# MLP's first weights and input made in the last group of the first attention, and another order of small work in the second attention

## The chip, the cores and the metric

One core of one Trainium2 chip runs the whole program in one launch. The metric is the device time of that launch in microseconds (us). Five engines work side by side and meet at semaphores: TensorE (PE; its weight loads are shown as PEld), VectorE (DVE), ScalarE (ACT), GpSimd (POOL) and SyncE (SP, which here only issues transfers).

## What is computed

Two transformer layers in fp32 on 2 x 1024 tokens of width 256. Each of the four parts has the same frame, x + layernorm(part(layernorm(x))):

```python
x = x + _layernorm(_L0_attn_ref(_layernorm(x), ...))   # 16 heads of 128, weights = codes * scales, full softmax
x = x + _layernorm(_L0_ffn_ref(_layernorm(x), ...))    # silu(x @ gate.T * gs) * (x @ up.T * us) @ down.T * ds, 704 hidden
x = x + _layernorm(_L1_attn_ref(_layernorm(x), ...))   # 16 heads of 16, causal softmax
x = x + _layernorm(_L1_ffn_ref(_layernorm(x), ...))    # 2 shared experts + top 8 of 16 routed ones, 128 hidden each
```

## The kernel before

**Precision.** A fp32 product is made from a high and a low part of each operand, in three matmuls (`three_passes`; `project` does it for both halves of the 256 channels). So each operand is split first: ACT copies it to its high part, then DVE (if the source is in PSUM) or POOL (if in SBUF) subtracts for the low part. `take_hi` and `take_lo` do it for the input of a stage, after `turn` on PE has transposed it.

**Norm.** The 16 tiles of 128 tokens are 4 groups of 4. For one group, a norm after a part is: statistics of the part's result `acc` (DVE, `stats_acc`), scale and offset (POOL, `scale_acc`), `normalise_acc` (ACT), add to x and statistics of x (DVE, `add_up`), `scale_x` (POOL), `normalise_x` (ACT), then `turn`, `take_hi`, `take_lo` into `xT`. norm1 stands between the first attention and the MLP, norm3 between the second attention and the experts.

**First attention** (`attention0_stage`). Two heads a pass, two sequences a pass. In the last one, norm1 of groups 0 and 1 is woven in by `begin_norm`; their x rows are loaded then, and the MLP's first 128 hidden units (`first_part`) with them. After the last tile PE runs `weighted_v` in four parts (o of the last group) with `output` of the group before between them. Then ACT and DVE split o, and `output` of the last group runs in two halves through one PSUM bank, bank 7. DVE does acc statistics of group 2 ahead of reading the first half (lines 960 to 964). The stage ends with a barrier of all engines.

**MLP** (`Mlp0.block`). 24 steps: 6 slices of 128 hidden units (`e`) for each of 4 token groups (`c`). PE runs `gate_up(s+1)` (12 matmuls of 512 columns), then `down(s)` (12 of 256). Ahead of the first, it turns input group 0, and ACT and DVE split it. Slices are split by `split_hi` (ACT) and `split_lo` (POOL), slices 0 and 1 first, slice s+2 in step s. Group 1 is turned in step 1, groups 2 and 3 in steps 6 and 10. Steps 7 and later carry parts of norm2 and the second attention's first projections (`Early`).

**Second attention** (`attention1_stage`). 8 halves (4 heads of one sequence each) of 12 quads; step g of 96 does quad g. In a step PE makes scores of quad g+2 into a ring of 4 PSUM banks, peaks for a later half into 3 other banks, and weighs v; ACT takes exp, DVE the peaks. `small_work` names by quad what else is done: `project`, `stack` (q and k spread to 64 rows; four a chunk of 512 tokens), `shift` (adds the peaks), `sums`, `spread` and `out` (end of a head group's result). Each of them takes one ring bank, in order, so it waits for what used this bank four places earlier. POOL's `make_y` (4 instructions) lies between spread and out.

**Experts** (`Moe`) begin inside the last steps: the router's logits, `sigmoid`, the best 8 (`find_best`, `take_best`), the weights (`weigh_best`, 7 small DVE instructions in a row); step p of the experts is g = TOTAL + p, and there PE runs `gate_up(p+1)` and `down(p)`, and DVE `product(p+1)` and `add_up(p)`, with `hidden_hi` (ACT) and `hidden_lo` (POOL) between.

## Time and profile before

| | |
|---|---|
| median of 3 runs | 2249.73 us (2246.76 to 2250.08) |
| profiled execution, its own time | 2251.21 us |
| its span, first to last instruction | 2249.5 us |
| mean granted TensorE clock | 0.971 |
| first attention, up to its last instruction | 1354.8 us |
| MLP, to the second attention's first matmul | 1355.2 to 1498.9 us |
| second attention, to its last o | up to 1900.3 us |

Of the profile, the page gives shares by engine, the timeline gives instructions of one engine in order of time, and the view of waits gives sums of them. In a timeline a line is: start (us), duration (us), engine, source line, operation, what it writes <- what it reads, sizes, count of merged instructions, and in brackets how long the engine stood idle before it and what ended that.

### The profile page before, as it was taken

To read this page: it belongs to the slowest core of one execution; us is meant where nothing else is said; L and a number is where in the kernel's file an instruction comes from. 1 tells how busy PE (TensorE), PEld (TensorE's weight loads), DVE (VectorE), ACT (ScalarE), POOL (GpSimd) and SP (SyncE) were. 2 spreads that over 40 slices of the span, in tenths; PEclk is the share of its full clock that TensorE was granted. 3 is DMA by queue.
4 is the path that set the end of the run, shared out by engine and by line. 5 is a ranking of instruction groups with operands and counts; after the bars stand their busy time and mean duration, and the time that the engine had idled before them with its cause. 6 is when DMAs were issued, how large, how long until landed. Compare 5 with 4: busy or idle time off the path is not lost. (4 is left out here: it accounts for less than half of the span.)

```text
span 2249.5 us, 35911 instructions
## 1 busy us (share of the span) xinstructions
PE 2122.8 (94%) x12680; PEld 1710.5 (76%) x12680; DVE 1468.5 (65%) x2625; ACT 1186.2 (53%) x2159; POOL 565.8 (25%) x558
## 2 busy tenths in 40 slices
PE   6999999999999999999999998989889898899996
PEld 5888888888888888888888877764455445788885
DVE  6676676676676676676667775446766782655555
ACT  5565465465465465455556555526656764433333
POOL 3021031031031031021021005412333443544443
PEclk9999999999999999999999998988999997999998
DMA  2010010010010010010020002000000010110001
GB/s 81 1 41 2 1 41 2 1 41 2 1 40 2 1 41 2 1 41 2 1 41 29 1 10 73 1 8 4 4 4 6 1 36 15 36 36 22 22 1 38
DMA packets 37687, 41.03 MB, mean 18 GB/s; under 512 B 7936, under 2 KB 33408, under 8 KB 37504
## 3 DMA queue, kind: packets, MB, share of 16 engines
q1 hardware_dynamic: 37504, 38.57, 6.4%
q8 instruction: 118, 1.93, 0.4%
q14 instruction: 65, 0.53, 0.1%
HBM read 36.45 MB, written 2.10 MB: 17 GB/s over the span
## 5 line engine op out<-in xcount | busy, mean ns | idle before, releaser
L816 ACT ACTIVATE attn_probT_hi<-psum 128x512 fp32r<-128x512 f32 x512 | 278.4, 595 | 305.9 <-PE psum L678 305.9
L874 DVE TENSOR_REDUCE attn_neg_max<-psum 128x1 f32<-128x1024 f32 x256 | 313.1, 1223 | 193.0 <-PE psum L81 192.4
L931 DVE TENSOR_TENSOR attn_probT_lo<-psum,attn_probT_hi 128x512 fp32r<-128x512 f32 x512 | 327.2, 680 | 28.0 <-ACT attn_probT_hi L816 27.9
L790 ACT ACTIVATE attn_prob<-psum,attn_neg_max 128x1024 f32<-128x1024 f32 x256 | 286.7, 1120 | 6.5 <-DVE attn_neg_max L874 6.5
L678 PEld LDWEIGHTS psum<-ident_sb,attn_prob 128*128 128x128 f32 x2048 | 237.8, 141 | 61.9 <-DVE attn_probT_lo L931 13.3
L678 PE MATMUL psum<-ident_sb,attn_prob 128*128 128x128 f32 x2048 | 267.4, 274 | 11.2 <-ACT attn_prob L790 11.2
L607 POOL TENSOR_TENSOR attn_v_lo<-x_sb,attn_v_hi 128x512 fp32r<-128x512 f32 x64 | 82.0, 1281 | 762.1 <-ACT attn_v_hi L824 762.1
L81 PE MATMUL psum<-attn_probT_hi,attn_v_hi 128*128 128x512 f32 x512 | 212.3, 415 | 0.6 <-DVE attn_probT_lo L931 0.6
L2216 ACT ACTIVATE attn_probT<-psum 128x512 f32<-128x512 f32 (+3 forms) x384 | 163.9, 495 | 92.2 <-PE psum L2101 89.2
L81 PE MATMUL psum<-attn_key_hi,attn_q_lo 128*128 128x512 f32 x512 | 201.0, 393 | 9.8 <-issue 9.8
L81 PE MATMUL psum<-attn_key_hi,attn_q_hi 128*128 128x512 f32 x512 | 201.4, 393 | 4.9 <-DVE xT_lo L348 4.9
L81 PE MATMUL psum<-attn_probT_lo,attn_v_hi 128*128 128x512 f32 x512 | 201.3, 393 | 0.0
L81 PE MATMUL psum<-attn_key_lo,attn_q_hi 128*128 128x512 f32 x512 | 200.7, 392 | 0.0
L81 PE MATMUL psum<-attn_probT_hi,attn_v_lo 128*128 128x512 f32 x512 | 200.4, 391 | 0.0
L1783 DVE TENSOR_REDUCE attn_peaks<-psum 128x1 f32<-128x512 f32 (+1 forms) x256 | 155.9, 651 | 47.7 <-PE psum L1747 26.0
L891 DVE SCALAR_TENSOR_TENSOR acc_sb<-psum,attn_over_total,acc_sb 128x256 f32<-128x256 f32 x256 | 111.7, 478 | 59.8 <-PE psum L81 54.1
L1422 POOL TENSOR_TENSOR attn_qk_lo<-attn_moe_hidden,attn_qk_hi 128x512 fp32r<-128x512 f32 x72 | 93.3, 1296 | 176.6 <-ACT attn_qk_hi L1386 176.6
L1449 DVE TENSOR_TENSOR attn_moe_hidden<-psum,attn_v 128x512 f32<-128x512 f32 x72 | 49.7, 690 | 134.0 <-ACT attn_v L1380 113.0
L81 PE MATMUL psum<-xT_hi,attn_q 128*128 128x512 f32 x288 | 116.8, 406 | 6.5 <-POOL attn_key L1418 6.5
L81 PE MATMUL psum<-xT_hi,attn_w_hi 128*128 128x512 f32 x288 | 117.3, 407 | 3.2 <-POOL attn_bias_v L560 2.1
L2101 PE MATMUL psum<-attn_q,attn_key 64*128 64x512 f32 (+3 forms) x384 | 106.1, 443 | 11.3 <-DVEq L2287 4.2
L1462 DVE SCALAR_TENSOR_TENSOR acc_sb<-psum,moe_weigh,acc_sb 128x256 f32<-128x256 f32 x272 | 112.9, 477 | 5.3 <-PE psum L81 5.1
(222 smaller groups left out, 4855.0 us busy)
## 6 DMA issues: line engine op xcount, KB each, us to landing
attn_v_all<-in_moe_w SPq DMA_DIRECT2D x23, 384.0 KB, 3.0
acc_sb<-in_x SPq DMA_DIRECT2D x4, 512.0 KB, 6.0
x_sb<-in_wq_codes SPq DMA_DIRECT2D x8, 256.0 KB, 2.5
x_sb<-in_wq_scales SPq DMA_DIRECT2D x32, 64.0 KB, 3.0
x_sb<-in_wk_codes SPq DMA_DIRECT2D x8, 256.0 KB, 3.8
x_sb<-in_wk_scales SPq DMA_DIRECT2D x32, 64.0 KB, 4.5
x_sb<-in_wv_codes SPq DMA_DIRECT2D x8, 256.0 KB, 5.1
x_sb<-in_wv_scales SPq DMA_DIRECT2D x32, 64.0 KB, 5.6
```

The source lines that it names most:

```text
L81: ins = nc.tensor.matmul(out, stationary[s], moving[m], start=start and n == 0, stop=stop and n == len(PASSES) - 1)
L678: mm = nc.tensor.transpose(ring(use)[:, j * P:(j + 1) * P], prob[:, i % 2, kt * P:(kt + 1) * P], k.ident[:])
L790: nc.scalar.activation(prob[:, i % 2, :], scores(i).rearrange("p a b -> p (a b)"), ACT.Exp, bias=neg_max[:, i % 2:i % 2 + 1], accum_out=to ...
L816: nc.scalar.activation(probT[0][:, g % 2, half_tile * GT:(half_tile + 1) * GT, j * P:(j + 1) * P], ring(use).rearrange("p (t n) -> p t n", ...
L874: nc.vector.tensor_reduce(neg_max[:, i % 2:i % 2 + 1], scores(i), AX.XY, ALU.max, negate=True).then_inc(max_ready, 1)
L891: add = nc.vector.scalar_tensor_tensor(out=to, in0=out_bank[:, j * C:(j + 1) * C], scalar=over_total[:, g * GT + t:g * GT + t + 1], in1=to ...
L931: nc.vector.tensor_tensor(to[1], ring(use).rearrange("p (t n) -> p t n", n=P), f32(to[0]), ALU.subtract).then_inc(ring_free, 1)
L1422: self.nc.gpsimd.tensor_tensor(self.hid[1][p % 2], self.hidden[p % 2], f32(self.hid[0][p % 2]), ALU.subtract).then_inc(self.lo_done, 1)
L1462: ins = self.nc.vector.scalar_tensor_tensor(out=acc, in0=self.down_tile(j), scalar=by, in1=acc, op0=ALU.mult, op1=ALU.add)
L1783: nc.vector.tensor_reduce(to[:, h:h + 1], bank[:, 0:width], AX.X, ALU.max, negate=True).then_inc(max_free, 1)
L2101: nc.tensor.matmul(score_bank(n)[:, q0:], key[half % 2][pair][rows(h), kt * P:(kt + 1) * P], q[half % 2][pair][rows(h), c * NB + q0:(c + 1 ...
L2216: nc.scalar.activation(probT[:, slot(g, h), q0:], score_bank(g * HG + h)[:, q0:], ACT.Exp, scale=float(D1) ** -0.5).then_inc(exp_done, 1)
```

## The change

What it does, in four parts.

1. *The last group of the first attention.* PE turns input groups 0 and 1 between the parts of `weighted_v`, into banks 2 to 5. ACT runs a Silu on a 128x1 tile, makes the high part of MLP slice 0 and takes the high parts of both input groups; DVE multiplies the down columns of slices 0 and 1 by their scale and takes the low parts; POOL makes the low part of slice 0. The parts of slice 0 lie in the still free columns of `xT`. Slice 1 is loaded where x of group 2 was. The last `output` uses a second bank, bank 1, for its second half. Norm1's acc statistics, scale and normalise of group 2 leave this stage.
2. *MLP.* PE begins with `gate_up(0)`. Slice 1 is split first, the permanent copy of slice 0 in step 4. Group 2's acc work comes to the beginning; x of groups 2 and 3 is loaded after the splits of slices 1 and 0; its steps move from X_ADD 1, 3 to 3, 7, the turns from 1, 6, 10 to 7, 11. SP issues the second attention's constants behind the load of group 3.
3. *Second attention.* The c = 1 stacks of the next half move from quads 2 and 3 to 0 and 1; the c = 0 projection of the half after it from quad 7 to 3, its weights' split from quad 2 to 1.
4. *Beginning of the experts.* Sigmoid from step 92 to 94, best from 93 to 95, weights from 94 to 97 (experts' step 1), `hidden_hi(0)` from 95 to 96, behind the last copy of o. `make_y` of the last chunk in two parts, two instructions in each of experts' steps 1 and 2.

```diff
@@ attention0_stage
+        out_bank, last_out_bank = k.psum[:, 7, :], k.psum[:, 1, :]
+        last_turn_banks = lambda g: k.psum[:, 2 + g * KC:2 + (g + 1) * KC, :]
...
-            ahead(sp)
+            mlp.load_first(sp)
             sp.wait_ge(v_done, passes * 2 * v_uses + 2)
-            for g in range(after.ahead, after.groups - 1):
-                after.load_x(sp, g)
+            mlp.load_second(sp)
...
-            after.early_gpsimd(pool, after.ahead)
+            mlp.first_lo(pool, first_hi)
...
                 for part in range(GT):
                     weighted_v(half, groups - 1, part)
+                    if beside:
+                        beside(part)
                     if 1 <= part <= 2:
                         output(half, groups - 2, part - 1)
+            def begin_mlp(part):
+                if part < after.ahead:
+                    after.turn(pe, part, last_turn_banks(part)).then_inc(after.turned, 1)
...
+            def begin_mlp():
+                nc.scalar.activation(neg_max[:, 0:1], neg_max[:, 0:1], ACT.Silu)
+                mlp.first_hi(act, first_scaled, first_hi)
+                for g in range(after.ahead):
+                    act.wait_ge(after.turned, g + 1)
+                    after.take_hi(act, g, last_turn_banks(g))
-            after.early_scalar(act, after.ahead)
...
                 for part in range(2):
                     add_up(half, b, groups - 2, part)
+                    if beside:
+                        after.take_lo(dve, part, last_turn_banks(part))
                 o_lo(half, groups - 1)
+                if i == tiles - 1:
+                    mlp.scale_first(dve, first_scaled)
-            after.early_vector(dve, after.ahead)
@@ Mlp0
+    def scale_first(self, dve, done):
+        self.scale_down(self.first_part, self.first_row).then_inc(done, 1)
+        self.scale_down(self.second_part, self.first_row)
+    def first_hi(self, act, scaled, done):
+        act.wait_ge(scaled, 1)
+        self.nc.scalar.activation(self.first_halves[0], self.first_part, ACT.Copy).then_inc(done, 1)
+    def first_lo(self, pool, hi_done):
+        self.nc.gpsimd.tensor_tensor(self.first_halves[1], self.first_part, f32(self.first_halves[0]), ALU.subtract)
...
-        X_ADD, X_STATS, X_ACT, X_TURN = {1: 2, 3: 3}, {2: 2, 5: 3}, {4: 2, 7: 3}, {1: 1, 6: 2, 10: 3}
+        X_ADD, X_STATS, X_ACT, X_TURN = {3: 2, 7: 3}, {4: 2, 8: 3}, {5: 2, 9: 3}, {7: 2, 11: 3}
+        SPLIT = {-1: 1, 0: 2, 1: 3, 2: 4, 3: 5, 4: 0}
...
-                for e in range(1, N):
+                for e in range(2, N):
                     sp.dma_start(staged[:, e - 1, :], self.w_dram[e]).then_inc(self.landed[min(e, 3)], 16)
+                sp.wait_ge(w_ready, 1)
+                before.load_x(sp, before.groups - 2)
                 sp.wait_ge(row_kept, 1)
-                sp.wait_ge(w_ready, 1)
+                sp.wait_ge(w_ready, N)
                 before.load_x(sp, before.groups - 1)
                 early.sync(sp)
...
-                turn(before, "x", 0)
                 gate_up(0)
@@ attention1_stage
-        1: [("shift", 0, 1, 0), ("sums", -1, 1, 0)],
-        2: [("spread", -1, 1, 0), ("stack", 1, 1, 0), ("stack", 1, 1, 1)],
-        3: [("stack", 1, 1, 2), ("stack", 1, 1, 3)],
+        0: [("stack", 1, 1, 0), ("stack", 1, 1, 1)],
+        1: [("shift", 0, 1, 0), ("sums", -1, 1, 0), ("stack", 1, 1, 2), ("stack", 1, 1, 3)],
+        2: [("spread", -1, 1, 0)],
+        3: [("project", 2, 0, 0)],
...
-        7: [("project", 2, 0, 0)],
...
-    LAST_Y, LAST_OUT = 1, 4
+    LAST_Y, LAST_OUT = (TOTAL + 1, TOTAL + 2), 4
-    ROUTER_AT, LOGITS_AT, SIGMOID_AT, BEST_AT, WEIGH_AT = 84, range(TOTAL - 8, TOTAL - 4), TOTAL - 4, TOTAL - 3, TOTAL - 2
+    ROUTER_AT, LOGITS_AT, SIGMOID_AT, BEST_AT, WEIGH_AT = 84, range(TOTAL - 8, TOTAL - 4), TOTAL - 2, TOTAL - 1, TOTAL + 1
...
-                if r == 2 and 0 <= half + 2 < HALVES:
+                if r == 1 and 0 <= half + 2 < HALVES:
                     split_weights(pool, half + 2)
...
-                if g == TOTAL - 1:
+                if g == TOTAL:
                     act.wait_ge(stacked, HALVES * chunks * 2 * pairs)
                     moe.hidden_hi(act, 0)
```

## Rows read from the trace of the kernel before

**Rows 1.** The page's first part: busy time, share of the span, instructions.
```profile
PE 2122.8 (94%) x12680; PEld 1710.5 (76%) x12680; DVE 1468.5 (65%) x2625; ACT 1186.2 (53%) x2159; POOL 565.8 (25%) x558
```

**Rows 2.** PE's timeline around the end of the first attention.
```profile
1349.28 0.38 PE L81 MATMUL psum<-attn_wo_hi,attn_o_hi 128*128 128x256 f32 x1 [1.41 <-DVE attn_o_lo L879]
1352.27 0.58 PE L81 MATMUL psum<-attn_wo_hi,attn_o_hi 128*128 128x256 f32 x1 [2.02 <-DVE acc_sb L891]
1355.16 1.94 PE L334 MATMUL psum<-ident_sb,acc_sb 128*128 128x128 f32 x8 [1.24 <-PEq L422]
1359.70 0.77 PE L81 MATMUL psum<-xT_hi,mlp_w_hi 128*128 128x512 f32 x1 [2.59 <-DVE xT_lo L348]
...
1374.32 1.03 PE L334 MATMUL psum<-ident_sb,acc_sb 128*128 128x128 f32 x8
```

**Rows 3.** Windows: length; busy PE, PEld, DVE, ACT, POOL; PEclk; DMA share; GB/s.
```profile
1347.87:1352.20 4.33, 0.97 (x7) 0.77 (x6) 3.56 (x14) 0.60 (x1) 0.89 (x1) 0.90 0.00 0
...
1359.70:1364.90 5.20, 5.20 (x12) 4.10 (x13) 0.18 (x1) 2.81 (x3) 1.97 (x3) 0.50 1.02 363
```

**Rows 4.** ACT's timeline around the same place.
```profile
1347.91 0.60 ACT L832 ACTIVATE attn_o_hi<-psum 128x512 fp32r<-128x512 f32 x1 [7.22 <-PE psum L81]
...
1357.20 1.02 ACT L339 ACTIVATE xT_hi<-psum 128x1024 fp32r<-128x1024 f32 x1
```

**Rows 5.** DVE's timeline around the same place.
```profile
1344.49 0.87 DVE L891 SCALAR_TENSOR_TENSOR acc_sb<-psum,attn_over_total,acc_sb 128x256 f32<-128x256 f32 x2 [2.42 <-PE psum L81]
...
1349.14 1.39 DVE L244 BATCH_NORM_STATS2 room_sb<-acc_sb 128x6 f32<-128x256 f32 x4
...
1358.33 1.23 DVE L348 TENSOR_TENSOR xT_lo<-psum,xT_hi 128x1024 fp32r<-128x1024 f32 x1 [2.08 <-ACT xT_hi L339]
```

**Rows 6.** PE's timeline in the MLP, its two waits between steps 3 and 5.
```profile
1384.08 0.74 PE L1090 MATMUL psum<-mlp_w_hi,mlp_hid_lo 128*128 128x256 f32 x4 [0.57 <-POOL mlp_hid_lo L1181]
...
1385.90 0.47 PE L81 MATMUL psum<-xT_hi,mlp_w_hi 128*128 128x512 f32 x1 [1.08 <-issue]
```

**Rows 7.** POOL's timeline in the MLP: a slice's low part, and scale_x of group 2.
```profile
1357.21 1.80 POOL L1172 TENSOR_TENSOR mlp_w_lo<-x_sb,mlp_w_hi 128x768 fp32r<-128x768 f32 x1 [1.57 <-ACT mlp_w_hi L1115]
...
1380.70 1.01 POOL L211 TENSOR_TENSOR room_sb<-room_sb 128x4 f32<-128x4 f32 x1 [2.23 <-DVE room_sb L252]
```

**Rows 8.** PE's waits in half 4 (1723.3 to 1765.9): total us, times, longest.
```profile
PE psum L1747 <- DVE attn_peaks L1783: 1.2, 3, 0.7
...
PE psum L1728 <- ACT attn_probT L2216: 0.5, 1, 0.5
PE psum L2101 <- ACTq L2243: 0.3, 1, 0.3
```

**Rows 9.** ACT's timeline at quads 0 to 2 of the same half.
```profile
1729.54 1.08 ACT L2216 ACTIVATE attn_probT<-psum 128x512 f32<-128x512 f32 x2 [1.49 <-PE psum L2101]
...
1732.75 0.60 ACT L1768 ACTIVATE attn_q<-psum 128x512 fp32r<-128x512 f32 x1
1733.47 0.69 ACT L1765 ACTIVATE attn_key<-psum,attn_ones_key 128x512 fp32r<-128x512 f32 x1
```

**Rows 10.** DVE's timeline there: the shift is added to both pairs.
```profile
1728.20 1.29 DVE L1810 TENSOR_TENSOR attn_q<-psum,attn_q 128x512 fp32r<-128x512 f32 x2 [0.35 <-PE psum L1736]
```

**Rows 11.** ACT's timeline at the last quads.
```profile
1890.58 1.28 ACT L1391 ACT_TABLE_LOAD   x1
...
1892.17 1.28 ACT L2216 ACT_TABLE_LOAD   x1
...
1899.68 0.58 ACT L2223 ACTIVATE attn_o<-psum 128x512 f32<-128x512 f32 x1
```

**Rows 12.** PE's timeline at the last quads and the experts' first steps.
```profile
1893.79 0.38 PE L81 MATMUL psum<-attn_wp_hi,attn_y_hi 128*128 128x256 f32 x1 [2.44 <-ACT attn_probT L2216]
...
1900.41 1.40 PE L2155 MATMUL psum<-attn_sum_rows,attn_o 128*128 128x4 f32 x8 [2.32 <-ACT attn_o L2223]
...
1923.98 0.39 PE L81 MATMUL psum<-attn_q,attn_qk_hi 128*128 128x256 f32 x1 [3.39 <-POOL attn_qk_lo L1422]
```

**Rows 13.** DVE's timeline: the sixth instruction of weigh_best.
```profile
1900.12 1.23 DVE L1490 TENSOR_TENSOR moe_rest<-moe_rest,moe_score 128x128 f32<-128x128 f32 x1
```

**Rows 14.** POOL's timeline in the experts' steps 2 and 3, behind make_y.
```profile
1922.66 1.27 POOL L1422 TENSOR_TENSOR attn_qk_lo<-attn_moe_hidden,attn_qk_hi 128x512 fp32r<-128x512 f32 x1
1923.88 1.02 POOL L211 TENSOR_TENSOR room_sb<-room_sb 128x4 f32<-128x4 f32 x1
```

More of the change, by code:

```diff
@@ L627, in _ @@
                 after.scale_x(pool, g)
-            after.early_gpsimd(pool, after.ahead)
-            after.done["gpsimd"] = after.ahead + 1
+            mlp.first_lo(pool, first_hi)
         @block.tensor
@@ L698, in weighted_v, with output @@
                     mm.then_inc(o_full, 1)
-            def output(half, g, part):
+            def output(half, g, part, last=False):
                 use = (half * groups + g) * 2 + part
@@ L704, in output @@
                     pe.wait_ge(o_done, half * groups + g + 2)
-                pe.wait_ge(out_done, use + 1)
+                if not (last and part):
+                    pe.wait_ge(out_done, use + 1)
+                bank = (out_bank, last_out_bank)[last and part]
                 for j in range(2):
                     t = part * 2 + j
-                    mm = three_passes(nc, out_bank[:, j * C:(j + 1) * C], [h[:, t * P:(t + 1) * P] for h in o],
+                    mm = three_passes(nc, bank[:, j * C:(j + 1) * C], [h[:, t * P:(t + 1) * P] for h in o],
                                       [h[:, g // QG, :] for h in wo])
@@ L879, in o_lo, with add_up @@
                 nc.vector.tensor_tensor(o[1][:], o_bank(g), f32(o[0][:]), ALU.subtract).then_inc(o_done, 1)
-            def add_up(half, b, g, part):
+            def add_up(half, b, g, part, last=False):
+                bank = (out_bank, last_out_bank)[last and part]
                 use = (half * groups + g) * 2 + part
@@ L957, in begin_norm @@
                     after.add_up(dve, NORM_X_DVE.index(i))
+                if i == tiles - 1:
+                    mlp.scale_first(dve, first_scaled)
             halves(dve, projections, attend, begin_norm)
[L960 to L962 removed]
             for part in range(2):
[L964 removed]
+                add_up(passes * BATCH - 1, BATCH - 1, groups - 1, part, last=True)
 def f32(ap):
@@ L1138, in take_hi @@
                     norm.take_hi(act, g, slot((kind, g)))
-                for e in range(2):
-                    split_hi(e)
-                    if e == 0:
-                        take_hi(before, "x", 0)
-                act.wait_ge(self.landed[0], 48)
+                split_hi(SPLIT[-1])
                 for s in range(STEPS):
```

110 lines of the change are left out of this document (65 added, 45 removed).

## The prediction

> **What bounds the kernel now.** I began with the page's busy times. PE is busy 94% of the span, and the next engine, DVE, 65% [rows 1]. So time can be won in three ways only: less PE work, PE's waits, or stretches in which PE runs at the lower of its two clocks. The change removes no PE work worth naming, so I looked for waits and clock where it cuts: PE's timeline at the end of the first attention, the windows there, the timelines of ACT and DVE for the cover, then a half of the second attention in the view of waits, and the first steps of the experts.
>
> At the end of the first attention PE waits 1.41 us for the low part of o, 2.02 us for bank 7 to be read, 1.24 us for the barrier and 2.59 us for the split of input group 0 [rows 2]. The second wait is long because DVE had begun group 2's statistics just ahead [rows 5]. Through these gaps (0.97 us of work in 4.33) the granted clock falls, and the first 12 matmuls of the MLP take 5.20 us at a granted clock of 0.50, which is 1.2 GHz; at 2.4 they would be half of that, 2.6 [rows 3]. The first MLP matmul starts at 1359.70 [rows 2].
>
> **Part 1, the way into the MLP.** *Added on PE ahead of the last output:* two turns. A turn costs about 1.0 us (1.03 us at full clock [rows 2], 0.99 from its start to the next matmul), so the low part of o comes 2 x 0.99 = 1.98 us later, and the output starts at 1349.28 + 1.98 = 1351.26. *Removed:* the wait for bank 7, since the second half has bank 1, and group 2's statistics in front of it. Both halves run in a row. Six matmuls of 256 columns take half of what 12 of 512 columns take in pairs: 5.20 / 4 = 1.3 us each half at the low clock [rows 3], 0.65 at the high one. They end at 1353.9 or 1352.6. DVE then adds the halves, 0.87 us for each [rows 5], the second behind PE's end or behind the first add: 1355.0 or 1354.2. Before, the last add ended at 1354.84 and PE went on at 1355.16 [rows 2], 0.32 us later. So PE starts its next work at 1355.3 (low clock) or 1354.5 (high), nearly as before; but now this is `gate_up(0)` and not a turn. Against 1359.70 that is **-4.4 us**, or -5.2.
>
> *What hides the moved work.* ACT stood idle 7.22 us before the last split of o [rows 4]. It gets a table load (1.28, the price in [rows 11]), slice 0's high part and two `take_hi` of 1.02 [rows 4], some 4.3 us, and 1.98 us more room. DVE stood idle 2.42 us before the first of the two adds [rows 5] and 1.16 before the second. It gets two multiplications of 0.4 us and two `take_lo` of 1.23 [rows 5], 3.3 us, into 3.6 + 1.98. The second `take_lo` ends about when ACT has split o, so it is the tightest place; if it is late, each us goes straight into the path. POOL is idle there. On SP, x of groups 2 and 3 and the second attention's constants now stand behind the splits of slices 1 and 0; their first readers are steps 3 and 6 to 8 of the MLP, 4.2 us a step, and I cost that at nothing. Without this cover it would be the landing time, some 5 us once.
>
> *Clock.* The gaps left are about 1.4 us before the output and 1.6 us after it, with 1.3 us of work between. That is nearest to the 4.33 us with 0.97 of work, after which the clock was low [rows 3], so I take the low clock, and the first 12 matmuls cost the same 5.2 us as before: 0. The other end is -2.6 us. The Trainium skill, in "TensorE: Matmul & The Clock Gate", section "What's actually happening", says that an idle array drops to 1.2 GHz and gets 2.4 back only after sustained work. The rows agree, and the rule supports the low end here.
>
> **Part 2, within the MLP.** The turn of group 1 leaves step 1: **-1.0 us** [rows 2]. Between steps 3 and 5 PE waits 0.57 + 1.08 us [rows 6]: POOL had stood idle 2.23 us in front of the scale of group 2 [rows 7], a wait for DVE's statistics, with a low part and a slice's split queued behind it. That scale moves to step 4, where the splits are through, so I take the whole **-1.65 us** (bounds -1.65 and 0). On the other side POOL has slice 1 and group 2's acc scale to do at the beginning. At the low clock `gate_up(0)` lasts 5.2 us, and POOL's 1.80 us [rows 7] behind ACT's 0.84 are hidden; at the high clock PE would catch up with POOL in steps 0 and 1 and wait about 1.4 us. So parts 1 and 2 give -4.4 - 1.0 - 1.65 = **-7.1 us** at the low clock and -5.2 - 2.6 - 1.0 - 1.65 + 1.4 = -9.1 at the high one.
>
> **Part 3, the second attention's halves.** At quads 2 and 3 ACT has the exps of 512 columns, four takes of stacks (0.60 and 0.69 us [rows 9]), the copy of spread and a copy of o; at quads 0 and 1 its exps are short and it waits, 1.49 us in one place [rows 9]. PE's waits that belong to the crowded quads are 0.5 and 0.3 us a half [rows 8]. Moving the stacks could remove 0.8 us in each of 7 halves, 5.6 us. The projection at quad 7 starves DVE of peaks, and PE pays with three waits of together 1.2 us right behind it [rows 8]; at quad 3 it may or may not do the same. That is up to 1.2 x 6 halves = 7.2 us. The ring costs something back: in quad 1 four banks are now taken by shift, sums and two stacks, so the next quad's first score waits for both pairs' shift instead of one, half of 1.29 [rows 10], 0.65 x 7 = 4.5 us. The ends are -12.8 and +4.5, and I take **-4 us**, their middle, since each of these waits is below 0.7 us and can come back at another place.
>
> **Part 4, the beginning of the experts.** Before, ACT loads the sigmoid's table and then loads the exp's again, 1.28 us each [rows 11], in front of the last exps; PE waits 2.44 us for them [rows 12]. Sigmoid now stands behind the last exp, so one load is gone and the other two lie beside PE's last outputs: -2.4 us. The last copy of o stood behind `hidden_hi(0)`, and that behind DVE's product and best; PE waited 2.32 us for it [rows 12], of which a copy's 0.58 [rows 11] and the semaphores (0.8 together) stay: -1.5. The experts so begin 3.9 us earlier. By the row a table load is 1.28 us and nothing more, as the next ACTIVATE starts at once. The Trainium skill, in "ScalarE: Activation LUTs", section "What ACT_TABLE_LOAD costs", puts a switch at about 2.66 us, of which 1.38 is a drain; by it this part would give 1.4 us more, but no such drain shows here.
>
> Then something is given back. `weigh_best` was done while DVE waited for PE; now it stands in front of `product(2)`. Its seven instructions take 1.8 to 2.8 us (the sixth took 1.23 alone [rows 13]). Everything behind it moves by some 2 us: the hidden parts of step 2, and DVE's x statistics of group 2. POOL's order is now hidden low part of step 3, scale of group 2 (waits for these statistics), then the second half of `make_y`, 2.3 to 3.1 us, on which PE's last outs wait. Before, the outs followed at once on PE's wait of 3.39 us [rows 12], because all of y was made first and the low part, 1.27 us, only after it [rows 14]. Adding up in this order I get outs 1.5 us later against the experts' new start than before. So part 4 is -3.9 + 1.5 = **-2.4 us**, with -7.3 (the 3.39 gone and nothing back) and +0.5 as ends.
>
> **Sum.** -7.1 - 4 - 2.4 = -13.5 us. The profiled execution took 2251.21 us with a span of 2249.5, so 1.7 us lie around the span; it stands 1.5 us above the median. The change moves the span alone, so the median goes from 2249.73 to **2236.2 us**.
>
> **The rivals.**
> *Only the way into the MLP pays.* The small waits in the halves come back elsewhere, and the experts' start is taken back in full by y: -7.1, 2242.6 us. For it: PE is 94% busy, and no wait of a half is above 0.7 us [rows 1, 8].
> *PE stays at the high clock and the waits really go.* -9.1, -6 in the halves and -5 at the experts: -20, 2229.7 us. Against it is the clock after a like gap [rows 3].
> *The ring turns the halves around, slower than before.* The stacks of quads 0 and 1 occupy ring banks that the scores of the next quad need, and these long scores feed all of ACT's exps. Each half then pays both takes of a stack pair, 0.60 + 0.69 with 0.27 between and behind [rows 9], the second shift's 0.65 [rows 10], and 0.45 for ACT being late: 2.66 us, 18.6 in 7 halves, and the sum is -9.5 + 18.6 = +9.1, 2258.8 us. It decides from 1.36 us a half. Against it: ACT is idle just there [rows 9].
> *DVE and POOL hold each other up.* One of `weigh_best`'s small instructions took 1.23 us [rows 13] beside a POOL instruction, where its neighbours took 0.2. In step 1 POOL is busier than where it stood. If three of the seven lose a POOL instruction's 1.27 us [rows 14], 3.9 us are added, and the time is 2240.1 us. The Trainium skill, in "SBUF — State Buffer", section "Who interferes with whom", has the rule for it, an exclusive lock on the port pair that the two share; it speaks against this step, and the row agrees.
> *The change doesn't do what it says:* the early Silu need not keep the compiler from loading the table again in the MLP. That would cost nothing, since ACT waits for PE there, so it is no case of its own.
>
> **How the numbers follow.** The forecast, 0.50; only the way in, 0.20; high clock, 0.17; the port, 0.08; the ring, 0.05. The forecast's own range is 2229 to 2243. The range for 8 in 10 goes from 2227 (past the second rival, without the two lower ends of parts 3 and 4 together) to 2244.5 (above the first rival), and leaves out the ring and some of the ends. A measurement of this kernel can tell some 0.2%, 4.5 us, from no change. Faster by more than that: 0.50 x 0.97 + 0.20 x 0.8 + 0.17 + 0.08 = 0.90. Within it: 0.05. Slower: the ring, 0.05.
>
> **What would show it right or wrong.** In the profile after: the first `gate_up` 4 to 5 us after the last output and no `take_lo` between them; PE's clock there; no wait of PE between steps 3 and 5 of the MLP, but perhaps one in steps 0 to 2; a half's length against 42.6 us for half 4, and which wait stands at quads 2, 3 and 7; one table load fewer; the first expert step 3.9 us nearer to the last scores; and what PE waits for before the last outs. The prediction is wrong if the halves grow, if `take_lo` of group 1 delays the last split of o, or if the outs wait much longer than 4 us for y.

## The result, and the profile after

The changed kernel takes **2230.46 us** (median of 4 runs, 2219.89 to 2235.59) against 2249.9 for the kernel before on the same chip: a ratio of 0.991 (95% interval 0.988 to 0.9935), about 20 us. The profiled execution took 2231.5 us with a span of 2229.7, so again 1.8 us lie around the span, and a granted clock of 0.975 (0.971 before). In the second set of runs below it was 2233.44 us, 0.9926 (0.990 to 0.995). The forecast was 2236.2 us, with a range from 2227.0 to 2244.5. One further execution of the kernel before took 4074.75 us at a mean granted clock of 0.513; no comparison below includes it.

The page of the changed kernel, first part, and the clock in 40 slices:

```profile
PE 2113.1 (95%) x12680; PEld 1707.6 (77%) x12680; DVE 1468.3 (66%) x2625; ACT 1186.4 (53%) x2160; POOL 568.0 (25%) x559
...
PEclk9999999999999999999999999999999998899998
```

PE has the same number of matmuls as in [rows 1], yet is busy 9.7 us less. So part of the gain is neither work nor waits but matmuls that run at the higher of PE's two clocks.

**The way into the MLP.** PE's timeline of the changed kernel, for [rows 2]:

```profile
1351.08 0.39 PE L81 MATMUL psum<-attn_wo_hi,attn_o_hi 128*128 128x256 f32 x1 [1.41 <-DVE attn_o_lo L895]
...
1354.15 0.47 PE L81 MATMUL psum<-xT_hi 128*128 128x512 f32 x1 [1.38 <-PEq L422]
...
1356.99 0.47 PE L81 MATMUL psum<-xT_hi,mlp_w_hi 128*128 128x512 f32 x1
```

Of the four waits two are left. Counted from the same matmul of the last group (1340.65 before, 1340.68 after), the MLP's first `gate_up` comes 19.05 us later before and 13.47 after; the traces of `halves`, `experts` and `stacks`, which leave this part alone, have 18.9 to 19.1, and those of `way_in`, `after_again`, `x3_earlier`, `y_first` and `both` 13.5. The first `gate_up` starts at 1354.15 and not at 1359.70, and its 12 matmuls take 2.84 us (to 1356.99) where [rows 3] had 5.20. The windows show the level, 1.00 up to 1365:

```profile
1351.00:1357.00 6.00, 4.55 (x25) 3.71 (x25) 4.55 (x17) 1.54 (x2) 2.36 (x2) 1.00 0.31 87
1357.00:1365.00 8.00, 6.99 (x34) 5.34 (x34) 6.08 (x16) 4.35 (x8) 5.66 (x8) 1.00 0.56 199
```

**Inside the MLP** the waits of [rows 6] are gone, but PE has three larger ones. PE's timeline at the `gate_up` of steps 2 and 3 and at the `down` of step 9:

```profile
1363.31 0.47 PE L81 MATMUL psum<-xT_hi,mlp_w_hi 128*128 128x512 f32 x1 [1.01 <-issue]
...
1368.55 0.47 PE L81 MATMUL psum<-xT_hi,mlp_w_hi 128*128 128x512 f32 x1 [0.78 <-issue]
...
1406.98 1.22 PE L1146 MATMUL psum<-mlp_w_hi,mlp_hid_lo 128*128 128x256 f32 x4 [2.66 <-POOL mlp_hid_lo L1235]
```

The first is the wait for slice 2. DVE, which multiplies it, waited for its DMA, and then the multiplication lasted three times as long as the next one:

```profile
1359.19 1.23 DVE L1021 TENSOR_TENSOR mlp_staged<-mlp_staged,mlp_row 128x256 f32<-128x256 f32 x1 [1.15 <-DMA mlp_staged<-in_ffn_w]
...
1364.55 0.41 DVE L1021 TENSOR_TENSOR mlp_staged<-mlp_staged,mlp_row 128x256 f32<-128x256 f32 x1
```

The second is the wait for slice 3's low part, which POOL makes from 1366.62 to 1368.45 right behind the hidden low part of step 1. That one was late by a chain on ACT: slice 2's high part (from 1360.46), then the normalise of group 2, which the change put there (2.06 us), and only then the Silu of step 1 (1363.18). So both go back to slice 2, but how late it comes differs between executions: `after_again`, the same kernel, has waits of 0.96 and 0.78 us here, `y_first` and `both`, which are the same up to this place, 0.19 us in all at slices 2 and 3.

The third is a queue on POOL: the scale of group 3 waits 3.96 us for its statistics, and the second attention's `wv` (1.04 + 2.13 us) stands behind it, ahead of the hidden low part that PE needs. POOL's timeline:

```profile
1400.87 1.21 POOL L211 TENSOR_TENSOR room_sb<-room_sb 128x4 f32<-128x4 f32 x1 [3.96 <-DVE room_sb L252]
...
1402.46 1.04 POOL L1756 TENSOR_TENSOR attn_wv_hi<-attn_in_wv,attn_one 128x512 fp32r<-128x512 f32 x1
1403.58 2.13 POOL L1758 TENSOR_TENSOR attn_wv_lo<-attn_in_wv,attn_wv_hi 128x512 fp32r<-128x512 f32 x1
1405.66 1.27 POOL L1235 TENSOR_TENSOR mlp_hid_lo<-mlp_hidden,mlp_hid_hi 128x512 fp32r<-128x512 f32 x1
```

**The halves.** PE's waits in half 4 of the changed kernel (1700.3 to 1741.8), for [rows 8]:

```profile
PE psum L1799 <- DVE attn_peaks L1835: 1.0, 2, 0.7
PE psum L2157 <- DVEq L2343: 0.9, 2, 0.7
PE psum L81 <- ACT attn_probT L2272: 0.2, 1, 0.2
```

Of the rows of quads 2 and 3 nothing is left, and of the three waits behind quad 7 one (with another for peaks); all waits of the half fall from 2.9 to 2.1 us, and the half from 42.6 to 41.5. I had not read half 2 before the prediction. It is worse than half 4; the kernel before, 1621.1 to 1675.6, then the changed one, 1606.3 to 1654.6:

```profile
PE psum L81 <- ACT attn_probT L2216: 2.6, 1, 2.6
PE psum L1747 <- DVE attn_peaks L1783: 1.8, 4, 1.0
PE psum L2101 <- DVEq L2287: 0.7, 1, 0.7
PE psum L1728 <- ACT attn_probT L2216: 0.5, 1, 0.5
```

```profile
PE psum L1799 <- DVE attn_peaks L1835: 1.0, 4, 0.4
PE psum L2157 <- DVEq L2343: 0.9, 2, 0.7
PE psum L81 <- ACT attn_probT L2272: 0.9, 1, 0.9
```

**The experts' beginning.** The waits of [rows 12] were 2.44, 2.32 and 3.39 us. Now the first is gone, the second is 1.21, and in place of the third there are two, 1.75 us for the hidden low part of step 3 and 2.90 for y's low part. In the view of waits (1500 to 1900) they are

```profile
PE psum L81 <- POOL attn_y_lo L2071: 4.4, 3, 2.9
...
PE psum L81 <- POOL attn_qk_lo L1471: 1.8, 1, 1.8
...
PE psum L2211 <- ACT attn_o L2279: 1.2, 1, 1.2
```

**Where the 19.8 us of span went.** The windows of the kernel before, then of the changed one: half 0, halves 1 to 7, and the rest.

```profile
1499.60:1571.20 71.60, 64.15 (x443) 37.48 (x441) 48.43 (x93) 38.52 (x80) 15.45 (x29) 0.84 0.03 9
1571.20:1899.70 328.50, 293.86 (x2266) 163.17 (x2262) 214.22 (x459) 211.64 (x456) 127.25 (x194) 0.94 0.04 11
1899.70:2249.50 349.80, 321.89 (x1804) 280.33 (x1804) 199.98 (x485) 125.92 (x203) 150.10 (x114) 0.96 0.08 25
```

```profile
1492.70:1556.70 64.00, 56.35 (x443) 32.87 (x441) 48.92 (x94) 38.35 (x79) 15.36 (x29) 0.97 0.04 10
1556.70:1873.40 316.70, 291.64 (x2268) 164.60 (x2262) 213.42 (x430) 209.39 (x454) 126.56 (x194) 0.94 0.04 12
1873.40:2229.70 356.30, 326.96 (x1804) 283.59 (x1804) 201.83 (x513) 126.44 (x204) 150.24 (x114) 0.94 0.08 24
```

Up to the second attention 6.9 us are gained (1499.6 against 1492.7), in half 0 7.6, in halves 1 to 7 11.8, and 6.5 are lost behind it. Half 0 has the same 443 matmuls and waits of about 7.5 and 7.3 us; what differs is the clock, 0.84 against 0.97. At the end PE stands idle 1.4 us more (27.9 before, 29.3 now), about the 1.26 us by which its waits grew there; the other 5.1 us are busy time at a lower mean clock, 0.94 against 0.96. In another execution of the same changed kernel (the run `after_again`) half 0 reads:

```profile
1493.60:1562.60 69.00, 63.06 (x443) 36.31 (x441) 48.94 (x94) 38.76 (x80) 15.37 (x29) 0.85 0.04 9
```

So the 7.6 us of half 0 in this pair of profiles are mostly one execution's clock, and no part of the change may be credited with them from one pair. For that many executions are needed.

### The profile page after: what moved, and what is told of

The parts are those of the page before. It is cut to its first block and busy times, and to the rows that moved or that the text cites. A ratio compares the mean times of both kernels' runs of the same rounds, so it can differ in the third digit from the quotient of the medians.

```text
span 2229.7 us, 35904 instructions
## 1 busy us (share of the span) xinstructions
PE 2113.1 (95%) x12680; PEld 1707.6 (77%) x12680; DVE 1468.3 (66%) x2625; ACT 1186.4 (53%) x2160; POOL 568.0 (25%) x559
## 5 line engine op out<-in xcount | busy, mean ns | idle before, releaser
L81 PE MATMUL psum<-xT_hi,attn_key 128*128 128x512 f32 x288 | 117.6, 408 | 0.0
L81 PE MATMUL psum<-xT_lo,attn_q 128*128 128x512 f32 x288 | 117.3, 407 | 0.0
```

The lines of the kernel that those rows point to most:

```text
L81: ins = nc.tensor.matmul(out, stationary[s], moving[m], start=start and n == 0, stop=stop and n == len(PASSES) - 1)
```

## The experiments

**How the runs are compared.** Every run gives its time and its mean granted clock, and the two go together: the 79 runs of the kernel before lie between 2236 us at 0.982 and 2269 us at 0.964. I fitted the 187 runs of all kernels with one level for each kernel and one slope for all. The slope is 1.55 us (± 0.08) for each 0.001 of mean clock, the runs scatter by 1.9 us around the fit, and the differences at an equal clock come out with ± 1.2 to 1.7 us (95%). "Clock" is what a kernel's own mean clock adds, "mean" the plain difference of the means:

```
kernel          runs  mean clock   at equal clock   clock   mean, all against before (2249.3 us, 0.9735)
way_in            12     0.9748     -2.4 +- 1.2     -2.0     -4.4
stacks            12     0.9713     -6.4 +- 1.2     +3.3     -3.1
halves            12     0.9737    -10.5 +- 1.2     -0.3    -10.8
experts           12     0.9737     -1.4 +- 1.2     -0.3     -1.7
changed kernel    10     0.9762    -14.6 +- 1.3     -4.2    -18.8
held              10     0.9757    -11.0 +- 1.3     -3.4    -14.4
held_filled       10     0.9784    -12.4 +- 1.3     -7.6    -20.0
x3_earlier         6     0.9768    -16.4 +- 1.6     -5.2    -21.6
y_first            6     0.9775    -16.0 +- 1.6     -6.2    -22.3
both               6     0.9792    -18.7 +- 1.6     -8.8    -27.5
both_filled        6     0.9792    -15.9 +- 1.6     -8.8    -24.7
filled_first       6     0.9803    -18.0 +- 1.7    -10.6    -28.6
```

The split has two limits. A wait that is removed can also raise the clock, and then its gain is partly in the clock column. And the clock column itself is uncertain: the mean clocks of the changed kernel and of the one before differ by 0.0027 ± 0.0026, so its -4.2 us are good to about ± 4. The runs come from several chips, with the kernel before run beside each.

### One part at a time

`way_in` is the kernel before with the whole of parts 1 and 2. `halves` has of the change only

```diff
-        1: [("shift", 0, 1, 0), ("sums", -1, 1, 0)],
-        2: [("spread", -1, 1, 0), ("stack", 1, 1, 0), ("stack", 1, 1, 1)],
-        3: [("stack", 1, 1, 2), ("stack", 1, 1, 3)],
+        0: [("stack", 1, 1, 0), ("stack", 1, 1, 1)],
+        1: [("shift", 0, 1, 0), ("sums", -1, 1, 0), ("stack", 1, 1, 2), ("stack", 1, 1, 3)],
+        2: [("spread", -1, 1, 0)],
+        3: [("project", 2, 0, 0)],
...
-        7: [("project", 2, 0, 0)],
```

with the weights' split in quad 1 and the projection for half 1 moved likewise, to five steps ahead of half 0. `experts` has only the following, with `make_y` in two parts:

```diff
-    LAST_Y, LAST_OUT = 1, 4
+    LAST_Y, LAST_OUT = (TOTAL + 1, TOTAL + 2), 4
...
-    ROUTER_AT, LOGITS_AT, SIGMOID_AT, BEST_AT, WEIGH_AT = 84, range(TOTAL - 8, TOTAL - 4), TOTAL - 4, TOTAL - 3, TOTAL - 2
+    ROUTER_AT, LOGITS_AT, SIGMOID_AT, BEST_AT, WEIGH_AT = 84, range(TOTAL - 8, TOTAL - 4), TOTAL - 2, TOTAL - 1, TOTAL + 1
...
-                if g == TOTAL - 1:
+                if g == TOTAL:
                     act.wait_ge(stacked, HALVES * chunks * 2 * pairs)
                     moe.hidden_hi(act, 0)
```

> The kernel before with parts 1 and 2 alone (the way into the MLP and the MLP's order); the second attention and the experts as before. Theory A (each part pays by its waits, and by the clock only at the way in): the second attention's first projection starts 6.9 us earlier, as in the changed kernel (1492.7 against 1499.6), and everything behind it keeps its length: -7 us. Theory B (the clock does half of it: PE was at its lower level for 130 us of the span before and 110 after, and where it falls depends on the gaps that precede, so the early part of the second attention profits too): -10 to -14 us, with half 0, 71.6 us before, down to some 64. Should the new 2.66 us wait of step 9 be caused by the MLP's own order, it is seen here too.

> The kernel before with part 3 alone (stacks of the later stack pair in quads 0 and 1, the projection in quad 3). Theory A: 0.8 to 1.0 us of PE's waits a half (half 4: 2.9 before, 2.1 after) for 7 halves, -5.5 to -7 us. Theory B: more than that by the clock, -9 to -13 us, because halves 0 to 3, which have the falls of the clock, lose them. Rival of the prediction (the ring turns the halves round): slower, up to +9.

> The kernel before with part 4 alone (sigmoid, best, weigh_best, hidden_hi and the last make_y in another order). Theory A: waits 2.44 + 2.32 + 3.39 become 1.2 + 1.75 + 2.9, so -2.3 us. Theory B: the two waits that stand 5 us apart there bring the clock down for longer (13.5 us more of it at the experts in the changed kernel, worth 6.7), so +2 to +5 us. Nothing at all if both are there in part.

> The changed kernel whole, beside its three parts on the same chip. By theory A it is the sum of the three, within 1.5 us: -7 -6 -2.3 = -15, and the rest of the -20 of the profile is chance in one execution's clock. By theory B the parts don't add up, since they share the stretches at the lower clock: the sum of the three differs by several us from -19.5.

Measured: `way_in` 2244.04 us, ratio 0.998 (0.996 to 1.000); `halves` 2240.81 us, 0.995 (0.993 to 0.997); `experts` 2248.79 us, 1.0005 (0.999 to 1.002); the whole 2233.44 us, 0.9926 (0.990 to 0.995); before 2250.6 us. At an equal clock the three parts (-2.4, -10.5 and -1.4 in the table) sum to -14.4 us (± 2.2), and the whole gives -14.6. So Theory A holds for all that isn't clock: **the parts add up**, to within ± 2.3 us. But neither theory had the sizes: the way in brings a third of what I thought, the halves twice. Theory B is right in that 4.2 us of the 18.8 stand in the clock column. It is wrong where it gave the clock a place: `halves` and `experts` leave the mean clock as it was, and `way_in` raises it by no more than runs scatter.

`way_in` also has the 2.66 us wait in step 9, so the MLP's own order makes it. Of the waits of 1.01 and 0.78 it has 0.15 in all: in that execution DVE didn't wait for slice 2's landing.

### Stacks or projection

`stacks` is `halves` with the projection left in quad 7 and its split in quad 2.

> The kernel before with the stacks of the later pair in quads 0 and 1 instead of 2 and 3, the projection left in quad 7. The two moves of part 3 together took 10.7 us at an equal mean clock (halves). Theory P (the stacks carry it: the waits of quads 2 and 3, in half 2 of before 0.47 + 0.29 + 2.62 us): -6 to -8 us at equal clock, half 4's waits 2.9 down to some 2.1 with the three of quad 7 (0.66, 0.27, 0.26) left. Theory Q (the projection carries it, by the three waits behind quad 7): -2 to -4 us.

Measured: 2244.78 us, ratio 0.9986 (0.996 to 1.001), and -6.4 us at an equal clock. The rest of `halves`, -4.1 (± 1.5), is then the projection's. That lies between the theories, nearer to P: both moves pay, the stacks more. The plain medians hide it, since this kernel's runs had the lowest clock of all (0.9713). In the view of waits over 1500 to 1900 of `stacks` the peaks (L1783) still cost 14.5 us in 34 waits:

```profile
PE psum L1747 <- DVE attn_peaks L1783: 14.5, 34, 0.8
```

against 15.1 in 32 in the kernel before, and 12.6 in 27 in `halves`. The move of the projection removes 1.9 us of these. It removes more in another place: half 2's wait for ACT in front of a projection, 2.62 us before (at 1642.57), is still there in `stacks` and shrinks only in `halves`. PE's timeline in `stacks`, then in `halves`:

```profile
1629.53 0.58 PE L81 MATMUL psum<-attn_wv_hi,xT_hi 128*128 128x256 f32 x1 [2.42 <-ACT attn_probT L2216]
```

```profile
1634.07 0.58 PE L81 MATMUL psum<-attn_wv_hi,xT_hi 128*128 128x256 f32 x1 [0.87 <-ACT attn_probT L2219]
```

Half 1's wait of 1.12 us does the same: 1.12 in `stacks`, 0.18 in `halves`. The two lines of quads 2 and 3 (L1728 behind ACT 3.4 us in 7 waits and L2101 behind ACTq 2.0 in 7) are gone from `stacks`, 5.4 us; 3.2 of them come back in front of the shift (L1736 behind ACT, 1.1 us before and 2.8 now, and behind DVE's `attn_shift`, none before and 1.5 now).

### The clock at the MLP's beginning

`held` makes the gap ahead of the MLP as long as it was before, and `held_filled` puts work that nobody needs into it (the lines with the loop are in it alone; in `held` the wait for `w_ready` keeps its place ahead of the one for `lo_done`):

```diff
-                    if not early_halves:
-                        pe.wait_ge(w_ready, splits_before[e] + 1)
...
                     pe.wait_ge(before.lo_done, (c + 1) * KC)
+                    if early_halves:
+                        for n in range(10):
+                            nc.tensor.matmul(slot(("step", s))[:, 0, :], k.xT[0][:, 0, 0:P], k.xT[0][:, 0, 0:NB],
+                                             start=True, stop=True)
+                    pe.wait_ge(w_ready, 1 if early_halves else splits_before[e] + 1)
```

> The changed kernel, but PE's first matmul of the MLP also waits until POOL has split slice 1, which ends at 1356.9: the gap ahead of it grows from 1.38 to some 4.3 us, as long as the wait and work of before (0.97 us of work in 4.33). Theory C (the clock at the MLP's beginning is decided by the length of PE's gaps there, and the prediction chose its level wrong because it counted gaps of 1.4 us as long): the granted clock is 0.50 in the first steps; the start is 2.9 us later, the first 12 matmuls take 5.2 instead of 2.8, and the waits of steps 2 and 3 (1.01 + 0.78) are covered: +3 to +4 us at the second attention's begin. Rival D (the level there comes from the work ahead, the two turns): the clock stays 1.0 and the second attention begins 1 to 2 us later.

> held, with ten matmuls of 512 columns (x's high half by itself, into the bank that the first gate overwrites) in the gap ahead of the wait for slice 1. The first real matmul of the MLP stays where it was, 2.9 us later than in the changed kernel. Theory C (an idle PE brings the level down, whatever it idles for): the clock stays at 1.0 there and the first 12 matmuls take 2.8 us instead of 5.2; at the second attention's begin 2.4 us are won against held, so +1 to +2 us against the changed kernel. If work that is thrown away doesn't hold the level: as held.

PE's timeline and the first 3.35 us of the MLP in `held`, then in `held_filled`:

```profile
1359.55 0.79 PE L81 MATMUL psum<-xT_hi 128*128 128x512 f32 x1 [4.14 <-POOL mlp_w_lo L1225]
...
1359.55:1362.90 3.35, 3.35 (x8) 2.67 (x9) 0.24 (x2) 0.39 (x1) 1.34 (x4) 0.50 0.93 329
```

```profile
1353.13 2.52 PE L1121 MATMUL psum<-xT_hi 128*128 128x512 f32 x10 [1.38 <-PEq L422]
1355.94 0.50 PE L81 MATMUL psum<-xT_hi 128*128 128x512 f32 x1 [0.29 <-POOL mlp_w_lo L1229]
...
1355.94:1359.30 3.36, 3.36 (x15) 2.77 (x16) 0.44 (x3) 0.69 (x1) 1.34 (x4) 1.00 0.91 306
```

In the same time 8 matmuls start in the one and 15 in the other. From the MLP's first matmul to the second attention's first projection `held` takes 139.6 us and `held_filled` 135.7, with 8.8 and 9.0 us of waits in the MLP: 3.9 us in this pair of traces, for the clock. The medians differ by 6.0 us and the means by 5.5 (± 4.6), nearly all of it in the clock column of the table. Theory C holds, rival D falls: at this place the level depends on whether PE stands still. The other traces agree: the first `gate_up` is at the lower level in the four kernels that have the old way in (`before`, `halves`, `experts`, `stacks`) and at the higher one in the eight traces that have the new one without `held`'s wait. Against the changed kernel `held` is 3.6 us slower at an equal clock (± 1.7; expected +3 to +4) and `held_filled` 2.2 (± 1.7; expected +1 to +2). The Trainium skill says of it, in "TensorE: Matmul & The Clock Gate", section "What's actually happening", that the low level is the default and activity releases it; these two traces agree, and in them the activity is work that nobody needs.

### Two waits that the change brought in

`x3_earlier`:

```diff
-        X_ADD, X_STATS, X_ACT, X_TURN = {3: 2, 7: 3}, {4: 2, 8: 3}, {5: 2, 9: 3}, {7: 2, 11: 3}
+        X_ADD, X_STATS, X_ACT, X_TURN = {3: 2, 5: 3}, {4: 2, 6: 3}, {5: 2, 7: 3}, {6: 2, 10: 3}
```

`y_first`, in POOL's order of the experts' step 2 (`Moe.gpsimd`, and its call):

```diff
         if p in self.split_at:
             self.split_lo(pool, self.split_at[p])
+        if beside:
+            beside()
         if p in self.ACC_DVE:
             self.norm.scale_acc(pool, self.ACC_DVE[p])
...
-                    moe.gpsimd(pool, g - TOTAL)
-                if g in LAST_Y:
-                    make_y(HALVES - 1, chunks - 1, (LAST_Y.index(g),))
+                    moe.gpsimd(pool, g - TOTAL, (lambda: make_y(HALVES - 1, chunks - 1, (1,))) if g == LAST_Y[1] else None)
+                if g == LAST_Y[0]:
+                    make_y(HALVES - 1, chunks - 1, (0,))
```

> The changed kernel with input group 3's add, statistics, scale and turn two steps (the turns one step) earlier in the MLP. The changed kernel's new wait, 2.66 us of PE in step 9 for a low part, stands on POOL behind the scale of group 3 (waits 3.96 us for DVE's statistics) and the second attention's wv (1.04 + 2.13). If that queue is its cause, it goes: -2.7 us, and up to -1.7 more for the fall of the clock that follows it; if the cause is wv alone, it stays above 1.5 us.

> The changed kernel, but at the experts' step 2 POOL makes the last high and low part of y ahead of the scale of group 2 and not behind it. In the changed kernel POOL waits 1.09 us for the statistics and takes 1.22 for the scale before y, and PE's last outs wait 2.90 us for y. If that order is what took back part 4's gain: the wait goes to some 0.6, -2.3 us, and -1 to -3 more if the clock stays up there. If the outs' wait only moves to the hidden low part of step 4, -1 us or less.

> The changed kernel with both mends, input group 3 earlier in the MLP and the last y ahead of the scale of group 2. At an equal mean clock the first gave -1.8 and the second -1.5 us against the changed kernel (each with an interval of some 2 us). If they are independent: -3.3 at an equal clock, some 2226 us; if the wait only moves on, no more than either of them.

`x3_earlier`: 2228.48 us (0.9905, 0.988 to 0.993). PE no longer waits in step 9; the MLP to the second attention's first projection takes 133.2 us against 138.5. Of the 5.3 us, 2.66 are this wait and 1.2 the waits at slices 2 and 3, which were smaller in this execution (0.62 in all); much of the rest is the clock, 0.99 against 0.96. POOL's order shows why: `wv` now stands behind a low part and not ahead of one.

```profile
1396.97 1.29 POOL L1235 TENSOR_TENSOR mlp_hid_lo<-mlp_hidden,mlp_hid_hi 128x512 fp32r<-128x512 f32 x1
1398.22 1.04 POOL L1756 TENSOR_TENSOR attn_wv_hi<-attn_in_wv,attn_one 128x512 fp32r<-128x512 f32 x1
1399.34 1.30 POOL L1758 TENSOR_TENSOR attn_wv_lo<-attn_in_wv,attn_wv_hi 128x512 fp32r<-128x512 f32 x1
1401.16 1.39 POOL L1235 TENSOR_TENSOR mlp_hid_lo<-mlp_hidden,mlp_hid_hi 128x512 fp32r<-128x512 f32 x1 [0.51 <-ACT mlp_hid_hi L1185]
```

`y_first`: 2226.61 us (0.990, 0.987 to 0.9925). The outs' wait is 0.50 and not 2.90:

```profile
1905.09 0.39 PE L81 MATMUL psum<-attn_q,attn_qk_hi 128*128 128x256 f32 x1 [1.75 <-POOL attn_qk_lo L1471]
1907.54 0.55 PE L81 MATMUL psum<-attn_wp_hi,attn_y_hi 128*128 128x256 f32 x1 [0.50 <-POOL attn_y_lo L2073]
```

Both explanations by a queue hold by their traces. Alone, neither gain can be told from none against the changed kernel (-1.8 and -1.4 us at an equal clock, ± 1.9 each). Together (`both`, 2220.9 us, 0.989, 0.986 to 0.992) they give -4.1 us (± 1.9) against the -3.3 expected if they add up.

### Filling two waits that stay

In steps 11 and 65 of the experts PE waits 3.28 and 3.17 us in the kernel before and in the changed one, and behind both waits the changed one was at the lower level. The kernel before and `both` were so only behind the one in step 65; behind the one in step 11 they stayed at the higher level. `filled_first` is `both` with twelve matmuls ahead of these waits; in `both_filled` the wait for `lo_done` stands ahead of the loop.

```diff
+        if p >= 2:
+            pe.wait_ge(self.prod_done, p - 1)
+        if p in (11, 65):
+            for n in range(12):
+                nc.tensor.matmul(k.psum[:, self.slots[p % 2][0], :], k.xT[0][:, 0, 0:P], k.xT[0][:, 0, 0:NB],
+                                 start=True, stop=True)
         pe.wait_ge(self.w_ready, v + 1)
         pe.wait_ge(self.norm.lo_done, (c + 1) * KC)
-        if p >= 2:
-            pe.wait_ge(self.prod_done, p - 1)
```

> both, and twelve such matmuls ahead of the wait for the weights' low part in the expert steps 11 and 65, where PE waits 3.28 and 3.17 us in every kernel and then works at the lower level for up to 6.8 us. Theory C: no wait gets shorter, but the level stays up behind it: 2.6 us in each place, -3 to -5 us against both, all of it in the mean clock and none at an equal clock. If the waits were too short to matter, or the level falls anyway: 0.

> both_filled, but in step 11 the filling matmuls stand ahead of the wait for x's low part, which was the true end of that gap, and not behind it (there they came on top: both_filled was slower than both by 2.8 us at an equal clock, what twelve matmuls take). Theory C: neither gap grows (both at an equal clock), and the level stays up behind the two: step 64 to 66 takes 12.0 us as in both_filled against 13.4 in both, steps 9 to 14 some 31 us against 34.1; 1.5 + 3 us against both, some 2217 us. If the level falls nonetheless, 2221 to 2222.

`both_filled` missed its forecast: 2223.87 us, and 2.8 us (± 2.2) slower than `both` at an equal clock. In step 11 the wait had been put down to POOL; the filling showed that it was for DVE's low part of x, so the filling began only when the wait was over, at the low level at that:

```profile
1933.54 5.49 PE L1369 MATMUL psum<-xT_hi 128*128 128x512 f32 x12 [3.23 <-DVE xT_lo L348]
```

In step 65 it did what it should. Windows from step 64 to 66 in `both`, then in `both_filled`:

```profile
2162.30:2175.70 13.40, 10.23 (x50) 8.56 (x49) 4.61 (x11) 3.26 (x6) 4.33 (x3) 0.87 0.00 0
```

```profile
2171.30:2183.30 12.00, 11.51 (x62) 9.58 (x61) 4.66 (x12) 3.32 (x6) 4.39 (x3) 1.00 0.00 0
```

With the filling ahead of both waits, `filled_first` took 2220.22 us (0.987, 0.984 to 0.989), at an equal clock +0.7 (± 2.2) against `both`, with a mean clock of 0.9803 against 0.9792. PE now waits 0.57 us in step 11, yet steps 9 to 14 took 37.2 us at a granted clock of 0.86 (34.1 at 0.95 in `both`). Against the 4.5 us that I expected, this is no difference that can be measured. The traces say why nothing could be won in step 11: in `both` the level hadn't fallen behind that gap (1.00 from 1930.27 to 1942), so the filling had nothing to hold. The fall comes later, and without a wait of PE. In `filled_first` it begins at about 1938.5, inside a run of 24 router matmuls of 16 columns each (from 1936.36, one every 0.11 us, then every 0.21). The row of PE's timeline, then the windows:

```profile
1938.50 0.34 PE L81 MATMUL psum<-moe_r_hi,xT_lo 128*128 128x16 f32 x1
```

```profile
1936.00:1940.00 4.00, 4.00 (x31) 3.90 (x30) 1.50 (x4) 0.53 (x1) 1.27 (x1) 0.82 0.02 4
1940.00:1944.00 4.00, 4.00 (x11) 3.13 (x10) 0.00 (x0) 0.60 (x1) 0.00 (x0) 0.50 0.00 0
```

A second fall stands near the end of the next such run, at about 1948.7, and in `both` the only one follows 1.3 us behind such a run. The profile counts PE as busy all this time. But the kernel before runs the same narrow matmuls from 1964.98 and 1971.90 and stays at the higher level. Filling can hold the level behind a gap (`held_filled`, step 65); whether the narrow matmuls bring it down, and why only in some executions, stays open.

## Why the prediction was right

**The first `gate_up`: right.** The output was to start at 1351.26 (1351.08), the last add to end at 1354.2 (1353.83) and the MLP's first matmul to start at 1354.5 for the high clock (1354.15). The second `take_lo`, the tightest place, ended at 1350.33, just when the split of o could begin. It came to -5.5 us, where I had given -4.4 for the low clock and -5.2 for the high one.

**The clock there: wrong.** I took the low level since "the gaps left are about 1.4 us before the output and 1.6 us after it", and called that near to 4.33 us with 0.97 of work. It was 1.00. `held` shows the size of the error: with a gap of 4.14 us it does fall, with two of 1.4 and their 1.4 us of work between it doesn't. The rival that took the high level had this term right (12 matmuls in 2.84 us).

**Part 2: the sign was wrong.** I took "the whole -1.65 us" for the waits between steps 3 and 5. They went, but 1.01 + 0.78 + 2.66 us came. The first two were in the text as the 1.4 us of catching up at the high clock, but their cause was another: POOL's catching up alone is worth 0.2 us (0.15 in `way_in`, 0.19 in `y_first`), the rest came from slice 2's landing, for which the sum had no term, and with it ACT's order in step 0. The 2.66 in step 9 I had not looked for: I followed group 2, and group 3 moved by three steps, from 5 to 8, ahead of `wv` on POOL. The steps of parts 1 and 2 together were to give -7.1 and gave -4.4 (± 3.7 by the scatter of the runs), of which 2.4 at an equal clock.

**Part 3: mis-sized.** -4 was the middle of -12.8 and +4.5, on the ground that each wait "is below 0.7 us and can come back at another place". It measured -10.5 (± 1.2), near the favourable end: stacks -6.4 against the 5.6 that I had as their most, projection -4.1 against at most 7.2. The step that failed is that I let half 4 stand for all ("no wait of a half is above 0.7 us"): half 2 has one of 2.6 us for ACT, which the stacks' move left at 2.4 and the projection's brought to 0.9, and half 1 one of 1.1, which fell to 0.2. The wait that I took back for the ring, for the second pair's shift, didn't appear (L2101 behind DVE's `attn_q` 1.5 us before, 0.8 in `halves`). Others at the ring did: in `halves` the shift's own matmuls wait 4.0 us and not 1.1, and the scores wait 6.1 us and not 4.2 for a bank that the projection holds. Together that is 4.8 us, about the size of the 4.5 that I took back, by another way. Summed in the view of waits over all eight halves, PE's waits fall from 39.6 us (1499.6 to 1899.7, without the 1.5 us that end before 1499.6) to 32.6 in `halves` (1501.3 to 1889.6), so 7.0 of the 10.5 us; the other 3.5 I can't place. Both stretches have 2704 matmuls and a mean granted clock of 0.92.

**Part 4: right.** -2.4 forecast, -1.4 (± 1.2) measured. The experts' begin is earlier by 2.44 + 1.11 us of waits, one table load of eight is gone, and (1.75 + 2.90) - 3.39 = 1.26 us are given back, against the 1.5 forecast, by the order that the text named; in `y_first`, with the order changed, the outs' wait is 0.50. But that the wait for a hidden low part goes beside it (1.75) I hadn't seen.

**The rivals.** The ring, as a rival that makes each half slower, falls: `halves` is 10.5 us faster. The port lock at `weigh_best` falls: its seven instructions took 0.17 to 0.38 us each (DVE's timeline, the sixth first), and the sixth took 0.29 in each of nine further traces with part 4:

```profile
1883.50 0.29 DVE L1539 TENSOR_TENSOR moe_rest<-moe_rest,moe_score 128x128 f32<-128x128 f32 x1
1883.82 0.38 DVE L1541 TENSOR_TENSOR moe_weigh<-moe_rest,moe_factor 128x128 f32<-128x128 f32 x1
```

Slice 2's multiplication is where it bit: 1.23 us beside a POOL instruction, 0.41 alone. The rule of the Trainium skill, in "SBUF — State Buffer", section "Who interferes with whom", that a DVE instruction with two inputs in SBUF contends with POOL's reads, fits with these rows.

**The rival that gave 2229.7 us**, the high clock with waits that really go, is nearer to the measured 2230.5 us than the forecast. It had the clock at the MLP right. But by its parts it isn't what happened: -9.1 for the way in (-4.4 measured), -6 in the halves (-10.5), -5 at the experts (-1.4).

**The sum.** -13.5 was forecast, and it is -14.6 (± 1.3) at an equal clock: the way in 4.7 us less, the halves 6.5 more, the experts 1.0 less. That the sum came out is in part luck, these errors cancelling. The other 4.2 us (± 4) stand in the clock column, for which the sum had no term beyond the MLP's beginning.

## What to carry to other kernels

Read the waits of each repetition of a loop, not of one that stands for all: the one with the large wait carries the gain. When a step moves, follow every group and every queue that moves with it, and ask what now stands ahead of the critical instruction on that engine. And where PE has two levels of clock, time a kernel over many executions and compare at an equal mean clock: here it cut the scatter from 5.7 us to 1.9 and showed parts of 2 us.

## What the runs showed of the hardware

- One kernel's time varies by 1.55 us for each 0.001 of mean granted clock, and its mean clock from 0.964 to 0.982 from one execution to the next, with no change in the program. Half 0 of the changed kernel took 64.0 us in one execution and 69.0 in another, with the same matmuls.
- A gap of 4.14 us ahead of the MLP brings PE to its lower level; two gaps of 1.4 us with 1.4 us of work between don't. Matmuls whose result nobody reads can hold the higher level: 3.9 us in the MLP (`held` against `held_filled`) and 1.4 us in the experts' step 65 (`both` against `both_filled`), one pair of traces each.
- The length of a gap alone doesn't settle the level: behind the same wait of 3.28 us in the experts' step 11 it fell in the changed kernel and stayed up in the kernel before and in `both`. And it can fall while PE counts as busy: in `filled_first` twice within runs of 24 matmuls of 16 columns.
- The releaser named for a wait on several semaphores can be one of two that end at nearly the same time: of the 3.28 us in step 11, POOL was named, and DVE's low part (in `both` from 1928.95 to 1930.18) was ready just before PE went on at 1930.27.
